# A transformer block's first batch: bias loaded as two rows, zeros multiplied at the start, work moved behind the first gate, and moving and stationary operands 64 bytes apart

## Time and profile before

| | |
|---|---|
| median of 3 runs | 1053.82 us (1053.54 to 1054.35) |
| profiled execution | 1054.15 us, of which the span is 1052.4 us |
| TensorE busy | 1028.3 us, 98% |
| VectorE busy | 785.5 us, 75% |
| ScalarE busy | 498.2 us, 47% |
| GpSimd busy | 211.7 us, 20% |
| DMA | 32.58 MB, 31 GB/s on the mean |

### The profile page before, as it was taken

The page is one execution under the profiler, slowest core; times in us unless marked ns, Lnnn a source line. Parts: engine busy times, 40 slices in busy tenths (PEclk is TensorE's granted clock), DMA queues, the critical chain, the costliest instruction groups (busy, mean ns, idle before and its releaser), DMA issues.

```text
span 1052.4 us, 18293 instructions
## 1 busy us (share of the span) xinstructions
PE 1028.3 (98%) x6672; PEld 934.5 (89%) x6672; DVE 785.5 (75%) x1782; ACT 498.2 (47%) x1117; POOL 211.7 (20%) x266
## 2 busy tenths in 40 slices
PE   6889999999999999999999999999999999999997
PEld 5879899988999899998999989999899988999986
DVE  5668886877768787778867778677786877767555
ACT  4445643455434653356534555255543465434332
POOL 0021122211221121221212211221122211222221
PEclk9979999999999999999999999999999999999999
DMA  5032000200011000110001100011000200000000
GB/s 178 11 112 81 2 21 1 82 21 2 21 42 61 1 2 21 42 60 3 1 21 42 61 2 21 1 59 43 2 21 2 82 21 3 21 2 22 2 21 21
DMA packets 13321, 32.58 MB, mean 31 GB/s; under 512 B 1840, under 2 KB 3632, under 8 KB 13232
## 3 DMA queue, kind: packets, MB, share of 16 engines
q1 hardware_dynamic: 13232, 31.42, 8.9%
HBM read 22.50 MB, written 8.39 MB: 29 GB/s over the span
## 4 chain that ended last, share of the span: by engine, by line
PE 96%; DVE 2%; ACT 1%; DMA 1%; issue 0%; SPq 0%; DVEq 0%
PE down_bank L1185 35%; PE up_bank L1185 34%; PE ring_bank L1185 9%; PE qk_bank L1185 8%; PE g_bank L1185 4%; PE ring_bank L1418 1%; PE ring_bank L1402 1%; PE g_bank L1229 1%; PE ring_bank L1425 1%; PE ring_bank L1424 1%; DMA sel_all<-in_b_qk 1%; PE ring_bank L1387 1%; DVE q L1057 0%; PE down_bank L1239 0%; PE ring_bank L1298 0%
## 5 line engine op out<-in xcount | busy, mean ns | idle before, releaser
L494 ACT ACTIVATE gated_h<-gated 128x512 fp32r<-128x512 f32 x256 | 161.5, 631 | 415.6 <-DVE gated L960 415.6
L480 POOL PARTITION_BROADCAST sel_all<-sel_rows x240 | 197.3, 822 | 726.5 <-DVE gated L960 725.6
L1185 PE MATMUL down_bank<-vals_h,gated_h 128*128 128x256 f32 x1024 | 294.8, 288 | 5.2 <-DVE gated_l L966 5.1
L1185 PE MATMUL down_bank<-vals_h,gated_l 128*128 128x256 f32 x1024 | 289.5, 283 | 0.0
L1185 PE MATMUL down_bank<-vals_l,gated_h 128*128 128x256 f32 x1024 | 289.3, 283 | 0.0
L960 DVE SCALAR_TENSOR_TENSOR gated<-up_bank,sel_all 128x512 f32<-128x512 f32 x256 | 176.1, 688 | 76.5 <-PE up_bank L1185 73.5
L966 DVE TENSOR_TENSOR gated_l<-gated,gated_h 128x512 fp32r<-128x512 f32 x256 | 173.3, 677 | 43.2 <-ACT gated_h L494 42.4
L1185 PEld LDWEIGHTS down_bank<-vals_h,gated_h 128*128 128x128 f32 x1024 | 194.5, 190 | 12.3 <-DVE gated_l L966 6.0
L1185 PE MATMUL up_bank<-x1T_h,keys_h 128*128 128x512 f32 x512 | 203.9, 398 | 0.0
L1185 PE MATMUL up_bank<-x1T_l,keys_h 128*128 128x512 f32 x512 | 203.3, 397 | 0.0
L1185 PE MATMUL up_bank<-x1T_h,keys_l 128*128 128x512 f32 x512 | 201.6, 394 | 0.0
(11 more groups left out here) (250 smaller groups left out, 1636.4 us busy)
## 6 DMA issues: line engine op xcount, KB each, us to landing
x_raw<-in_x SPq DMA_DIRECT2D x16, 512.0 KB, 4.6
out<-z SPq DMA_DIRECT2D x32, 256.0 KB, 2.3
xT_raw<-in_xT SPq DMA_DIRECT2D x14, 512.0 KB, 3.8
w_room<-in_keys SPq DMA_DIRECT2D x4, 512.0 KB, 3.8
z<-in_values SPq DMA_DIRECT2D x4, 512.0 KB, 4.7
xT_raw<-in_xT SPq DMA_DIRECT2D x4, 256.0 KB, 4.1
sel_rows<-sel SPq DMA_DIRECT2D x64, 8.0 KB
x<-in_wqk SPq DMA_DIRECT2D x2, 256.0 KB, 4.1
```

Of the source, the lines that this page charges most:

```text
L480: nc.gpsimd.partition_broadcast(sel_all[:, e % 2], row, P).then_inc(sel_spread, 1)
L494: return nc.scalar.activation(dst, src, ACT.Copy, **kw)
L1185: last = mm(dst, lhs, rhs, start=start and i == 0, stop=stop and i == n - 1, **kw)
```

## The change

It has four parts.

1. The start. The bias of q and k is loaded twice: first as two rows, on partitions 0 and 64, into a room that GpSimd has set to zero (`bias_row_raw`), and later in full (`bqk_raw`) for the steps of the later batches. `bias_hl` then holds the high part in row 0, the low part in row 64, and zeros elsewhere; the scale of 2/P goes. VectorE centres the two rows ahead of everything else, and ScalarE rounds them ahead of the key weights. The full bias is centred at the end of `first_batch`.
2. Zeros multiplied. TensorE runs six fp32 matmuls of 256 columns (`ones` x `esel_h`, which is zero then) before `keys0(0)`.
3. Order. On SP: x in three loads (tiles 0-1, 2-3, 4-7), `load_xT0(2)` ahead of the query weights, the small constants behind `load_xT0(3)`, `b_ln` behind piece 0, the full bias behind a wait for `wvl_made`. The low part of piece 0 moves from behind the second pair of layer norms to the middle of the key totals, that of piece 1 from behind the gate's logits to before them. The query scales are made for two tiles at a time. `queries0(1)` moves behind `q0_transpose(0)`, `queries0(2)` behind two transposes of x1, `queries0(3)` into step 0; the squares, scales and bias additions of tiles 4 to 7 move behind the gates of steps 0 to 2. The two halves of each key total are added on VectorE (`k_fold`), which halves the matmuls of `column_sums`. QT, Y and XT of tiles 4 to 7, and some QK, GG and LG stages, come one to three steps later.
4. Layout. Tensors are declared in a new order: moving operands first, then a filler of 64 bytes (`half_line`), then stationary operands, then the rest.

```diff
+WARM = 6
+LINE = 128
 FIRST_PLAN = {
-    0: [], 1: [("QT", 2)], 2: [("QT", 3)], 3: [("Y", 4)], 4: [("Y", 5)], 5: [("Y", 6), ("XT", 4)],
-    6: [("Y", 7), ("XT", 5)]}
+    0: [], 1: [], 2: [], 3: [("QT", 2)], 4: [("QT", 3)], 5: [("Y", 4)], 6: [("Y", 5)],
+    7: [("Y", 6), ("XT", 4), ("QK", 0)], 8: [("Y", 7), ("XT", 5), ("QK", 1)], 9: [("XT", 6), ("GG", 0)],
+    10: [("XT", 7), ("QK", 2), ("GG", 1)], 11: [("QK", 3)], 12: [("GG", 2), ("QK", 4), ("LG", 1)]}
-PIECE_STEPS = ((0, 0), (0, 1), (0, 4), (0, 6), (0, 8), (0, 10))
-PIECE_LO_STEPS = ((0, 1), (0, 2), (0, 5), (0, 7), (0, 9), (0, 11))
-PIECE_LOADS = ((0, 1), (0, 2), (0, 4), (0, 6), (0, 8))
+PIECE_STEPS = ((0, 1), (0, 2), (0, 4), (0, 5), (0, 7), (0, 9))
+PIECE_LO_STEPS = ((0, 2), (0, 3), (0, 5), (0, 6), (0, 9), (0, 10))
+PIECE_LOADS = ((0, 0), (0, 2), (0, 3), (0, 5), (0, 6))
...
+        half_line = sb("half_line", [P, LINE // 8])
...
             sp.dma_start(wqk_raw[:, :, 1], wqk[:, :, 1]).then_inc(w_k_in, 16)
             load_xT0(0)
-            sp.dma_start(bqk_raw, b_qk.partition_broadcast(P)).then_inc(bias_in, 16)
+            sp.wait_ge(constants_set, 1)
+            sp.dma_start(bias_row_raw[0:P:P // 2], b_qk.partition_broadcast(2)).then_inc(bias_row_in, 16)
             load_xT0(1)
...
+            sp.wait_ge(wvl_made, 1)
+            sp.dma_start(bqk_raw, b_qk.partition_broadcast(P)).then_inc(bias_in, 16)
             sp.wait_ge(piece_lo, 1)
             load_piece(2)
...
-                act.wait_ge(constants_set, 2)
+                act.wait_ge(constants_set, 3)
                 nc.scalar.activation(table_ahead[:, 0:1], eps_ln[:], sqrt)
+                act.wait_ge(qk_bias_set, 2)
+                copy(bias_hl, qk_bias[:]).then_inc(bias_hi, 1)
                 w_hi(1, 1)
                 xT_pair_hi(0)
-                act.wait_ge(qk_bias_set, 2)
-                copy(bias_hl, qk_bias[:], scale=2.0 / P).then_inc(bias_hi, 1)
...
+                if (it, s) == (0, 0):
+                    x0_bias(2)
+                elif (it, s) == (0, 1):
+                    q0_lift(GT, T)
+                    x0_bias(3)
+                elif (it, s) == (0, 2):
+                    q0_scales(GT, T, 3)
...
+                def k_fold():
+                    dve.wait_ge(k0_summed, 3)
+                    dve.wait_ge(k0_fourth_summed, 3)
+                    for total in (k0_fourth_total, k0_total):
+                        V.tensor_tensor(total[:, 0], total[:, 0], total[:, 1], ALU.add).then_inc(k0_folded, 1)
+
+                qk_bias_centred(bias_row_raw, bias_row_in, 1)
                 w_centre(1, 1, w_k_in)
...
+                pe.wait_ge(constants_set, 4)
+                for n in range(WARM):
+                    mm(ring_bank[n % 2][:, 0:M * P], ones[:], esel_h[:].bitcast(F32).rearrange("p m n -> p (m n)"),
+                       start=True, stop=True)
                 keys0(0)
                 keys0(1)
...
                 g0(3)
-                queries0(1)
                 y0_of_x(0)
                 y0_of_x(1)
                 column_sums()
                 kv0()
+                q0_transpose(0)
+                queries0(1)
                 y0_of_x(2)
+                y0_of_q(0)
+                y0_of_q(1)
                 y0_of_x(3)
-                q0_transpose(0)
                 q0_transpose(1)
-                for a in range(GT):
-                    y0_of_q(a)
+                y0_of_q(2)
+                y0_of_q(3)
+                x1_transpose(0)
+                x1_transpose(1)
                 queries0(2)
-                for a in range(GT):
-                    x1_transpose(a)
-                    if a == 1:
-                        queries0(3)
+                x1_transpose(2)
+                x1_transpose(3)
                 logits0()
...
                 layer1(it, s)
+                if (it, s) == (0, 0):
+                    queries0(3)
```

More of the change, by code:

```diff
@@ L706, in first_batch @@
                                              bias=eps_ln[:]).then_inc(y_rooted, 1)
-                    if p == 0:
-                        for m in range(M):
-                            act.wait_ge(kv0_scaled, m + 1)
-                            copy(kvw_h[:, m], kvw0[:, m]).then_inc(kv_hi, 1)
                     for a in (2 * p, 2 * p + 1):
@@ L1192, in _, with qk0, queries0 @@
             ALL = slice(None)
[L1194 to L1207 removed]
+            def qk0(bank, p, a):
+                cols = slice(a * C, (a + 1) * C)
+                for i in range(2):
+                    h, n = divmod(2 * p + i, GT)
+                    product(bank[:, i * C:(i + 1) * C],
+                            [(both(xT_h, xT_l, ALL, h, m, slice(n * P, (n + 1) * P)),
+                              both(wqk_h, wqk_l, ALL, m, cols)) for m in range(M)],
+                            start=i == 0, stop=False, skip_group_check=True)
+                pe.wait_ge(constants_set, 5)
+                pe.wait_ge(bias_lo, 1)
+                return mm(bank[:], ones_r, bias_hl[:, cols].unsqueeze(1).broadcast_to((P, 2, C)),
+                          start=False, stop=True, skip_group_check=True)
+            def queries0(p):
+                pe.wait_ge(wqk_lo, 2 * M)
+                if p == 1:
+                    pe.wait_ge(k0_squared, 2 * 3)
+                elif p == 2:
+                    pe.wait_ge(kv0_summed, M)
+                elif p == 3:
+                    pe.wait_ge(q0_copied, 2)
+                qk0(q0_bank(p), p, 0).then_inc(q0_projected, 1)
+            def first_batch():
                 def keys0(p):
@@ L1256, in column_sums @@
                             j = 2 * (n * M + m)
-                            for i in range(2):
-                                last = mm(cols0_place[:, j:j + 2], total[:, i, m * P:(m + 1) * P],
-                                          ones[:, 0:2], start=(i == 0), stop=(i == 1))
+                            last = mm(cols0_place[:, j:j + 2], total[:, 0, m * P:(m + 1) * P],
+                                      ones[:, 0:2], start=True, stop=True)
                     last.then_inc(cols0_summed, 1)
```

276 lines of the change are left out of this document (131 added, 145 removed).

## The result

The changed kernel takes 1029.74 us, the median of four runs (1028.76 to 1031.95), against 1053.78 before: a ratio of 0.9774, with a 95% interval of 0.9757 to 0.9791. That is 24.0 us; 6.4 were forecast. The profiled execution took 1028.76 us around its span of 1027.0.

What follows compares the result with a forecast made beforehand. TensorE, busy 98%, was taken as the bound, with avoidable waits and low clock in the first 63 us. Terms -5.1 - 2.0 + 0.7 = -6.4 gave 1047.4 us; 8 in 10 range 1025 to 1053.5.

Steps and rivals of the forecast that it cites:

- the layout: Operand addresses of the matmuls: moving and stationary operands 64 bytes apart were taken to have no effect, 0 us.
- rival B: Layout pays too: matmul spacing falls to 113 and 227 ns, 34 us in all; 1013 to 1043, middle 1030; chance 0.25.
- The page's gap: Matmul spacing by the page's N/2.4 + 2.5 ns: 109 and 216 ns; the forecast did not lean on it.
- The start: Up to the third key pair: first product 2.1 us later, third key pair 1.7 us earlier.
- I take it as warm: TensorE's clock stays up over 2.4 us of nothing behind the zeros; if cold, +1.6 us at most.
- Rival C: Gain given back: two bias rows land at 8.4, or later steps wait 3 us; 1050.5 to 1053.5; chance 0.13.
- The middle: Column sums, query pairs and layer norms up to the logits: logits at 48.0 instead of 51.3, -3.3 us.
- the gate: From logits to first `down`: TensorE bounds, the 4.36 us wait goes, `down` at 57.3; -5.5, less QT 2: -5.1.
- The clock falls there as it does now: At the logits TensorE's clock drops as before the change, with the same cost on both sides.
- TensorE's own order: Behind the logits, TensorE's work until 57.3 sets the first `down`, while the gate chain allows about 56.
- The second cold stretch: Half clock from 62.8 to 67.6 us, behind the wait for the gate, goes: -2.0 us.
- What comes back: Waits in later steps, where moved VectorE work lacks layer-1 cover: +0.7 us, bounds 0 and 3.

Runs made afterwards that it cites:

- e2: Kernel before with the new declaration order and the 64-byte filler, nothing else: 1037.58 us, ratio 0.9845.
- e4: Changed kernel with a filler of 32 bytes instead of 64: 1046.42 us, ratio 0.9929.
- e5: Changed kernel with a filler of 96 bytes instead of 64: 1046.89 us, ratio 0.9932.
- e1: Changed kernel with the declaration order of the kernel before and no filler: 1046.52 us, ratio 0.9928.
- e6: Changed kernel with `up` and wqk x xT (512 columns) at address difference 0, the 256-column pairs left at 64: 1038.04 us, ratio 0.9844.
- e11: Changed kernel with `down` alone moved to address difference 0: 1044.75 us, ratio 0.9914.
- e16: Changed kernel with the two bias rows centred behind the low part of x's first quarter, and wqk x xT at address difference 0: 1029.76 us, ratio 0.9771.
- e9: Changed kernel with the two bias rows centred and rounded behind the low part of x's first quarter: 1028.50 us, ratio 0.9758.
- e12: Changed kernel with each 512-column `up` product split into two of 256 columns: 1030.3 us, ratio 0.9786.
- e15: Kernel before with `down` alone at address difference 64: 1044.03 us, ratio 0.9903.

## Why the prediction was wrong

**The step that failed is the layout: "By the nearest rows, then, no effect: I take 0."** It measures 16.6 us (e2 against before). In the working of rival B the term is 3072 x 6 + 1536 x 6 and the rest. The runs give 3072 x 4.5 ns = 13.8 us for `down`, about 3 for Y's products (some 740, by 3 to 5 ns), 1.3 for x.T @ k2 (336 by 3.9), and nothing for the 512-column ones, which get 0.4 ns wider (-0.6 over 1536). That is 17.5, about what was measured. The trace of before had pairs at 0 and 32 and both cost 119; the step went on from there to 64, and e4 and e5 show why that was wrong: 0, 32 and 96 are alike, and 64 is a case of its own. What the trace did show was the wandering between 0.11 and 0.12, rival B's argument, and B was given a chance of 0.25. By B's reckoning (113 ns for 256 columns, half of it 17 us, middle 1030) the result is almost exact in time, but by luck: B's 34 us had the 512-column products in it as well, and they gave nothing, and the half of it that is its middle was a share without a reason. (The range was said to start at the middle of B, which is 1030; the figure given is 1025.)

The rule of the Trainium skill in "TensorE: Matmul & The Clock Gate" (Part 2, step 1: two independent read ports, so that loading weights takes nothing from the running matmul) says the same as the forecast's 0 (which didn't lean on it), and the measured time goes against both: the spacing of the same products changes with where the weights lie relative to the moving operand (119.0 to 114.5 ns, e2). That it is the two reads that disturb each other isn't shown, since every product here has a weight load of its own. The page's gap, 109 ns for 256 columns, is reached by neither layout.

**The start held in the profiled run, partly by luck.** Bias rows forecast at 4.6, came at 4.28; first product 9.35, came at 8.95, warm; ScalarE on the query weights 14.0, 13.98; third key pair 17.5, 17.47; column sums 0.95 us for eight, as forecast. But 4.28 is the second earliest of eleven landings, whose middle one is 5.21. And "I take it as warm" came true in two of nine such executions: the gap, forecast at 2.4 us, was 1.73 here, and in the seven with gaps of 2.01 to 3.93 the clock fell. Rival C's mechanism, everything behind one small load, is real and small: the landing moves by 1.7 us between executions and takes the first batch along.

**The middle and the gate were better than forecast.** Logits forecast 48.0, came at 46.58. "The clock falls there as it does now" failed in the profiled run: it stayed at 1.00. It isn't settled by that run: of the thirteen profiled executions with the new order it fell at the logits in seven and stayed up in six. In e1 it did fall (0.53 in 47.9 to 51.3), but was back at 1.00 in 51.3 to 57.3, where before it was 0.50. `down` forecast at 57.3 came at 53.51 (e1: 54.31). With query pair 3 at 2.4 GHz (49.02 to 50.40, 1.4 us where 2.9 were reckoned), TensorE's own order ends at 52.2, so that it isn't the bound as forecast: the gate chain is, with 1.3 us of waiting. (In e1, where the clock fell, the two end almost together: no wait for `gated_l` is listed there.)

**The second cold stretch went**, as forecast by 2.0: from the first to the second `down` e1 takes 2.93 us (54.31 to 57.24) and before took 5.42 (62.81 to 68.23, with 0.36 for QT 3): 2.1 us less for the same work.

**What comes back** was forecast at 0.7: one wait of 0.62 us for the scaled q at QT 2 (59.92) and one of 0.6 for the low part of k2, 1.2 in all. Start, order and gate together measure 7.7 us by the medians (e1 against before) against 6.4 forecast: the smaller miss. Within e1's profiled execution the first `down` comes 8.5 us earlier (5.5 forecast) and the second cold stretch gives 2.1, less 0.44 for QT 2: 10.2. Its span is 8.7 us shorter (1043.7 against 1052.4), so that 1.5 us come back, not 0.7. The gate was the term sized too small, what comes back the one that partly made up for it.

## What to carry to other kernels

When a kernel is bound by back-to-back matmuls, the start addresses of the two operands are a parameter of it: try the four differences of 0, 32, 64 and 96 bytes, which costs one filler and no instruction, before counting on any of them. Move all pairs together: one pair left at another difference can slow those behind it (e6, e11, e16). An operand layout for which the trace has no row is unknown, not zero; where the rows wander for no visible reason, that is a hint of something to be won or lost (here, between 0.11 and 0.12 us, it was). And ask of a small load at the head of an engine's queue how much later it may land: here it moved by 1.7 us between executions, and the first batch with it. Moving it back cost nothing (e9, 1028.50 us); that it makes the runs steadier isn't shown. What one profiled execution shows of the clock in the first 60 us isn't the kernel's: look at several.

## What was not expected of the hardware

- Products of 256 columns have two spacings at 2.4 GHz, 113 to 114 and 118 to 120 ns. Whole runs at the narrow level were seen only where moving and stationary operand start 64 bytes apart modulo 128. The means of 512-column products stay within 229 and 234 ns whatever the difference.
- At 64 there is a second level, 118 ns, and the products ahead have a part in which one a run takes (e6, e12, e15, e16); a rule that gives it for every run wasn't found. What inside the core holds this, and why 64, isn't shown by any run; that the reads of weights and of moving columns disturb each other in some rhythm is only argued.
- Matmuls of zeros raise the clock as others do: the products after them come at 0.12 us in the changed kernel, behind 1.73 us of nothing. In e6, where the two rows landed later and TensorE did nothing for 3.60 us, the first product takes 0.55 us and the next come 0.21 apart, as at 1.2 GHz, so a late landing also takes the zeros' worth away. Timeline of TensorE in e6:

```profile
10.31 0.55 PE L1210 MATMUL qk_bank<-wqk_h,xT_h 128*128 128x256 f32 x1 [3.60 <-DVE xT_l L1034]
10.67 0.41 PE L1210 MATMUL qk_bank<-wqk_l,xT_h 128*128 128x256 f32 x1
10.88 0.41 PE L1210 MATMUL qk_bank<-wqk_h,xT_l 128*128 128x256 f32 x1
```
